# A windowed attention block with routed experts: the mask of the scores, the residual sum and the experts' gathers moved between PE, VectorE, GpSimd and the DMA queues

## The chip, the cores and the metric

The kernel runs on one core of one Trainium2 chip. The metric is the device time of one execution in microseconds (us). PE is the matmul engine (TensorE), DVE is VectorE, ACT is ScalarE, POOL is GpSimd, SP is SyncE, whose work here is to issue DMA transfers.

## The reference

`x` has shape (8, 512, 256), float32. The block computes `x + s * g`, with `xn` the layer norm of `x`:

```python
qkv = (xn @ qkv_w.T)                    # 32 heads of 8
attn = q @ k.T * 8**-0.5                # per head
m = (8 - |i - j| / 2) / 8 where i - 8 <= j < i + 8, else 0
attn = softmax(where(m != 0, attn * m, -inf))
s = (attn @ v) @ proj_w.T + proj_b
logits = xn @ router_w                  # 8 experts
e = argmax(logits); score = sigmoid(max(logits))
routed = (silu(score * xn @ gate_w[e]) * (score * xn @ up_w[e])) @ down_w[e]
shared = silu(xn @ shared_gate_w) * (xn @ shared_up_w) @ shared_down_w
g = silu(routed + shared)
out = x + s * g
```

## The kernel before

The 4096 tokens are 32 tiles of 128 rows (`T`). The whole work is one loop over steps n = 0 to `LAST` = 66, written out by hand once for each engine; each engine works through its own list in order, and semaphores join the lists. A step n < `U` = 64 is the attention of 64 queries (two blocks of 32) for all heads. Its parts lie in three steps: in step n PE makes the scores (`scores`, L902), DVE multiplies them by the distance weight out of PSUM into one of three buffers `Sx` (`weigh`, L711) and takes the row maximum (`largest`, L721), and GpSimd subtracts it (`subtract`, L422). In step n + 1 ACT takes the exponential (`exps`, L495) and DVE transposes the result in 32 x 32 blocks (`flipped`, L742). In step n + 2 PE multiplies by v (`weighted`, L930), DVE inverts the sums (`invert`, L751), ACT copies the result out (`o_out`, L500), and DVE divides and transposes (`divide`, `turned`). v goes through DRAM: SP writes it (`keep_v`) and reads it back, spread over partitions, as `VB` (`spread_v`, L318, four transfers for a step).

The mask is added by PE: `scores` first multiplies an identity by a bf16 table of 0 and -3e38 (L912), one matmul for each half of the channels, and then adds the scores to it in PSUM (L916). `mask_kind(n)` picks the table for the first, inner and last blocks of a sequence.

Other work is placed by step number. The shared expert takes steps 0 to 5 of each eight (`sg`, `su`, `sg`, `su`, `sd`, `sd` in `jobs_of`, L113); a step with `sg` is called a gate step in this text: in it DVE waits for ACT's tanh. Steps 8 to 10 do the routing, and from step 10 (`SENT`) to 16 GpSimd scatters five tiles of scaled rows a step to `xs_dram`, sorted by expert (L419). From step 18 (`E0`) to about 39 two tiles of 128 rows a step go through their expert (`expert_rows`, `expert_up`, `expert_down`, for DVE `gate` and `gated`), and the results go to `ys_dram`. The four PSUM banks `psM` are used in turn by all these jobs, in the order of `ORDER`.

From step 40 (`C_STEP`) on, the 4096 rows are put together in 16 chunks c of two tiles (`CT`, `NC`). GpSimd gathers a chunk's expert rows into one of three buffers Y (`gather`, L428: two indirect DMAs), three chunks ahead, and adds them to the shared expert's rows (`combine`, L440). ACT takes tanh (`silu`, L549), DVE finishes the silu (`silu`, L792), multiplies it with the attention's output (`result`, L803) and adds `x` (L806), which SP has loaded again into a buffer XR (`load_x`), and SP stores XR to `out` (`store`). `silu_at(n)` and `result_at(n)` give the chunks of a step: a chunk a step from 41 and 42 on until chunk 12 (steps 53 and 54), then chunks 13 (54, 58), 14 (61, 62) and 15 (62, 66).

In SP's list a step goes: stores and loads of x, blank rows of `xs_dram`, loads of expert rows, of weights, `keep_v`, `spread_v`.

## Time and profile before

| | us |
|---|---|
| median of 3 runs | 641.51 (639.12 to 642.87) |
| the profiled execution | 641.16 |
| its span, first to last instruction | 639.3 |

| engine | busy us | share of the span | instructions |
|---|---|---|---|
| PE | 562.8 | 88% | 3358 |
| DVE | 404.0 | 63% | 853 |
| ACT | 308.1 | 48% | 762 |
| POOL | 186.8 | 29% | 160 |

Busy time is the time in which an engine had an instruction in work; issuing a DMA from SP or ACT, waits and branches don't count, but GpSimd's indirect DMAs do, since GpSimd writes their descriptors itself. Matmuls are pipelined, and their ends are modelled: what one costs is better read from the distance between the starts of neighbours. A row of a timeline merges like instructions that follow each other (x2, x4); in brackets stands how long the engine was idle before, and what released it. A span average hides that each part of the loop has its own limit, so the stretches have to be read one by one.

### The profile page before, as it was taken

The page shows a single profiled execution, that of the slowest core. Times are in us where ns is not written, and L with a number is a line of the kernel's source. Part 1 is how long each engine was busy: PE and PEld are TensorE (multiplying, and loading weights), DVE is VectorE, ACT ScalarE, POOL GpSimd, SP SyncE. Part 2 cuts the span into 40 slices and gives each one's busy share as a digit, 9 for nine tenths or more (in the row PEclk, how much of TensorE's full clock was granted, in tenths as well). Part 3 has the DMA queues.
Part 4 walks back from the last instruction along what each step waited for, and adds up shares of the span by engine and source line. Part 5 has one row for each costly group of instructions (what it writes and reads, how often), then busy time and mean ns, then how long its engine had stood idle before and what let it go on. Part 6 is the DMA issues. An engine that isn't in the chain of part 4 may idle for free. (4 is left out here: it accounts for less than half of the span.)

```text
span 639.3 us, 10599 instructions
## 1 busy us (share of the span) xinstructions
PE 562.8 (88%) x3358; PEld 484.0 (76%) x3358; DVE 404.0 (63%) x853; ACT 308.1 (48%) x762; POOL 186.8 (29%) x160
## 2 busy tenths in 40 slices
PE   2879999969879999999999999999886868789865
PEld 1657888858757899898999898898775756677754
DVE  6655746886755455455455455456688888886773
ACT  1374654557773544543544634546454543635332
POOL 6000101147861011010010110014645545532230
PEclk9899999979998999999999999999989899989997
DMA  9415532112326667666567576443133333330110
GB/s 294 133 62 190 177 122 61 57 44 96 111 87 178 174 166 223 196 184 195 165 189 223 167 218 185 134 133 107 51 98 110 102 106 105 113 109 20 43 35 23
DMA packets 107370, 82.89 MB, mean 130 GB/s; under 512 B 42292, under 2 KB 104756, under 8 KB 107316
## 3 DMA queue, kind: packets, MB, share of 16 engines
q1 hardware_dynamic: 98628, 68.72, 36.6%
q0 software_dynamic: 3072, 8.39, 4.1%
q10 hardware_dynamic: 5616, 5.11, 2.3%
q8 instruction: 27, 0.44, 0.3%
q14 instruction: 27, 0.22, 0.1%
HBM read 59.12 MB, written 23.07 MB: 129 GB/s over the span
## 5 line engine op out<-in xcount | busy, mean ns | idle before, releaser
L425 POOL TENSOR_TENSOR Sx<-Sx,mx 128x752 f32<-128x752 f32 x64 | 93.7, 1464 | 414.9 <-DVE mx L725 414.8
L941 PE MATMUL psV<-VB,PTs 128*128 128x132 f32 x1024 | 137.3, 288 | 43.3 <-DMA VB<-v_dram 19.0
L941 PEld LDWEIGHTS psV<-VB,PTs 128*128 128x128 f32 x1024 | 130.1, 197 | 50.8 <-issue 50.0
L468 ACT ACTIVATE Or<-psV 32x128 f32<-32x128 f32 x256 | 68.5, 268 | 151.4 <-DVE rs L755 148.9
L916 PE MATMUL psS<-kBD,qBD 128*128 128x188 f32 x512 | 104.9, 329 | 0.0
L916 PEld LDWEIGHTS psS<-kBD,qBD 128*128 128x128 f32 x512 | 87.9, 195 | 10.8 <-issue 2.0
L747 DVE STREAM_TRANSPOSE PTs<-Sx 128x512 f32<-128x512 f32 x128 | 82.9, 685 | 1.0 <-ACT Sx L498 1.0
L991 PE MATMUL psM<-xT,EB 128*128 128x128 f32 x624 | 76.4, 276 | 0.0
L718 DVE TENSOR_TENSOR Sx<-psS,cst 128x752 f32<-128x752 f32 x64 | 59.7, 933 | 26.3 <-PE psS L916 26.2
L991 PEld LDWEIGHTS psM<-xT,EB 128*128 128x128 f32 x624 | 73.9, 192 | 2.1 <-ACT qBD L487 1.3
L732 DVE SCALAR_TENSOR_TENSOR ea<-et,psM 128x256 f32<-128x256 f32 x39 | 16.4, 421 | 76.3 <-PE psM L991 47.2
L968 PE MATMUL psM<-xnT,wsgu 128*128 128x512 f32 x128 | 63.1, 617 | 0.0
L725 DVE TENSOR_REDUCE mx<-Sx 128x16 f32<-128x752 f32 x64 | 59.9, 936 | 2.2
L468 ACT ACTIVATE kBD<-psM 32x272 f32<-32x272 f32 x128 | 49.2, 385 | 17.1 <-PE psM L898 15.9
L498 ACT ACTIVATE Sx<-Sx 128x752 f32<-128x752 f32 x64 | 53.0, 828 | 4.9 <-POOL Sx L425 4.5
L764 DVE TENSOR_TENSOR O<-Or,rs 128x128 f32<-128x128 f32 x64 | 23.6, 369 | 41.3 <-issue 38.5
L487 ACT ACTIVATE qBD<-psM,cst 128x512 f32<-128x512 f32 x64 | 38.7, 688 | 21.7 <-PE psM L893 21.6
L912 PE MATMUL psS<-maskb,identb 128*128 128x376 bf16 x128 | 42.0, 328 | 6.7 <-DVE Sx L718 3.9
L949 PE MATMUL psM<-wp,OT 128*128 128x256 f32 x128 | 33.7, 386 | 3.8 <-DVE OT L772 2.3
L1000 PE MATMUL psM<-EB,ehT 128*128 128x256 f32 x156 | 36.9, 379 | 0.0
L968 PEld LDWEIGHTS psM<-xnT,wsgu 128*128 128x128 f32 x128 | 23.3, 201 | 17.0 <-issue 16.9
L927 PE MATMUL psM<-wqkv,xnT 128*128 128x264 f32 x128 | 31.0, 390 | 5.6 <-DVE ag L779 2.8
(107 smaller groups left out, 690.6 us busy)
## 6 DMA issues: line engine op xcount, KB each, us to landing
EB<-in_L_ffn_gate_w SPq DMA_DIRECT2D x39, 256.0 KB, 3.0
EB<-in_L_ffn_up_w SPq DMA_DIRECT2D x39, 256.0 KB, 3.5
EB<-in_L_ffn_down_w SPq DMA_DIRECT2D x39, 256.0 KB, 3.1
VB<-v_dram SPq DMA_DIRECT2D x256, 32.0 KB
stage<-xs_dram SPq DMA_DIRECT2D x39, 128.0 KB, 2.2
ys_dram<-yb ACTq DMA_DIRECT2D x39, 128.0 KB, 3.1
xs_dram<-blank SPq DMA_DIRECT2D x9, 512.0 KB, 3.1
v_dram<-vS SPq DMA_DIRECT2D x8, 512.0 KB, 3.0
```

What stands on the lines that cost most here:

```text
L425: nc.gpsimd.tensor_tensor(s, s, mx[n % 3][:, :].unsqueeze(2).broadcast_to([P, 2 * G, KW]), ALU.subtract).then_inc(a_sub, 1)
L468: return nc.scalar.activation(dst, src, ACT.Copy)
L487: last = nc.scalar.activation(qBD[h % 2][:, :, :, i, :], q, ACT.Copy, scale=cst[:, C_HEAD + i:C_HEAD + i + 1])
L498: nc.scalar.activation(s, s, ACT.Exp).then_inc(a_exp, 1)
L718: tt(s, psS[:, :, 0:BW].rearrange("p j (g k) -> p j g k", k=KW), mw.unsqueeze(1).unsqueeze(1).broadcast_to([P, 2, G, KW]), ALU.mult).then_ ...
L725: reduce(mx[n % 3][:, :], Sx[n % 3][:, :, 0:KW], AX, ALU.max).then_inc(a_max, 1)
L747: last = nc.vector.transpose(PTs[n % 2][:, k, :, :, :].rearrange("p j i (r q) -> p (j i r) q", q=QB), Sx[n % 3][:, :, k * QB:(k + 1) * QB])
L912: mm(psS[:, j, 0:BW], identb[:, :], maskb[:, kind:kind + 2, :, :].rearrange("p i r k -> p (i r k)"), start=True, stop=False)
L916: last = mm(psS[:, j, i * HS * KW:(i + 1) * HS * KW], qBD[h % 2][:, j, k, :, :].rearrange("p s q -> p (s q)"), kBD[h % 2][:, j, :, k * QB: ...
L941: last = mm(psV[:, j, at:at + HS * VW], PTs[n % 2][:, k, j, i, :], VB[n % 2][:, i, k, :, VW * j:VW * j + VW], start=k == 0, stop=k == 1)
L968: last = mm(ps[:, :], wsgu[:, kc, at:at + P], xnT[:, b, kc, WIN:WIN + SEQ], start=kc == 0, stop=kc == KC - 1)
L991: last = mm(ps[:, f * P:(f + 1) * P], egu[:, i % 2, kc, f * P:(f + 1) * P], xT[:, i % 2, kc, :], start=kc == 0, stop=kc == KC - 1)
```

## The change

1. `masked_late(n)` is true for steps 0 to 7 and 18 to 63. In those, `scores` leaves the mask matmuls out, and GpSimd adds the mask to `Sx` in SBUF (`banded`), between `weigh` and `largest`. The table for it, 12 x 47 columns, is part of the constants loaded at the start. In those steps DVE's `largest(n)` moves behind `flipped(n-1)`.
2. `out` is set to `x` by eight transfers from DRAM to DRAM (`preset`, 512 KB each, steps 8 to 15). `load_x`, `store`, the buffers XR and DVE's addition are gone; GpSimd issues a transfer for each chunk that adds the product to `out` (`add_out`, 256 KB), a step after its `result`, the last one in step 66.
3. The gathers add straight to the shared expert's rows; `combine` is gone. `gather(c)` stands in the step before its `silu`, behind `subtract`, and waits for the shared rows; ACT's `silu` waits for the gather.
4. In SP's list `spread_v(n-1)` stands first in its step, from step 10 on.

```diff
--- before.py
+++ after.py
@@ -64,7 +64,8 @@
 C_M = C_ID + P
 C_BIAS = C_M + KW
 C_HEAD = C_BIAS + C
-C_STAY = C_HEAD + HS
+C_BAND = C_HEAD + HS
+C_STAY = C_BAND + 12 * KW
 C_TRI, C_ONE = C_STAY, C_STAY + P
 C_FIRST = C_ONE + P
 C_TILE = C_FIRST + E
@@ -89,6 +90,7 @@
     key = np.arange(KW)[None, :]
     kinds = (band & (key >= WIN), band, band, band, band, band & (key < QB + WIN))
     c[:, C_MASK:] = np.concatenate([np.where(k, 0.0, NEG) for k in kinds], 1)
+    c[:, C_BAND:C_STAY] = np.tile(c[:, C_MASK:].reshape(P, 3, 1, 2 * KW), (1, 1, KC, 1)).reshape(P, 12 * KW)
     return c
 
 
@@ -98,6 +100,10 @@
 
 def mask_kind(n):
     return 0 if n % UB == 0 else 2 if n % UB == UB - 1 else 1
+
+
+def masked_late(n):
+    return n < BATCH or n >= E0
 
 
 def first_key(n):
@@ -211,9 +217,9 @@
         at += NT * E
         rcst = EB[:, at:at + C_END - C_STAY]
         Y = [EB[:, i * CT * C:(i + 1) * CT * C] for i in range(3)]
-        XR = [EB[:, (3 + i) * CT * C:(4 + i) * CT * C] for i in range(3)]
 
         ident = cst[:, C_ID:C_ID + P]
+        band = cst[:, C_BAND:C_BAND + 12 * KW].rearrange("p (m k) -> p m k", k=KW)
         mw = cst[:, C_M:C_M + KW]
         bias = cst[:, C_BIAS:C_BIAS + C]
         tri = rcst[:, C_TRI - C_STAY:C_TRI - C_STAY + P]
@@ -238,15 +244,15 @@
             sem("r_" + n) for n in ("sc", "tanh", "sce", "oh", "cnt", "slot", "row", "tab"))
         r_scat = [sem(f"r_scat{i}") for i in range(SENDS)]
         m_full = [sem(f"m_full{i}") for i in range(MB)]
-        a_qk, a_S, a_mul, a_max, a_sub, a_exp, a_PT, a_V, a_PV, a_O, a_rec, a_nrm, a_OT, a_s = (
-            sem("a_" + n) for n in ("qk", "S", "mul", "max", "sub", "exp", "PT", "V", "PV", "O", "rec", "nrm", "OT", "s"))
+        a_qk, a_S, a_mul, a_add, a_max, a_sub, a_exp, a_PT, a_V, a_PV, a_O, a_rec, a_nrm, a_OT, a_s = (
+            sem("a_" + n) for n in ("qk", "S", "mul", "add", "max", "sub", "exp", "PT", "V", "PV", "O", "rec", "nrm", "OT", "s"))
         x_v, x_vd = ([sem(f"x_{n}{i}") for i in range(2)] for n in ("v", "vd"))
         f_tg, f_ag, f_hT, f_sh = (sem("f_" + n) for n in ("tg", "ag", "hT", "sh"))
         b_in, b_wd, b_st = ([sem(f"b_{n}{i}") for i in range(k)] for n, k in (("in", 4), ("wd", 2), ("st", 3)))
         b_wg = [sem(f"b_wg{i}") for i in range(2)]
         b_xT, b_et, b_ea, b_hT, b_y = (sem("b_" + n) for n in ("xT", "et", "ea", "hT", "y"))
-        d_y, d_x, d_st = ([sem(f"d_{n}{i}") for i in range(3)] for n in ("y", "x", "st"))
-        d_z, d_t, d_w, d_g, d_o = (sem("d_" + n) for n in ("z", "t", "w", "g", "o"))
+        d_y, d_st = ([sem(f"d_{n}{i}") for i in range(3)] for n in ("y", "st"))
+        d_t, d_w, d_g, d_pre = (sem("d_" + n) for n in ("t", "w", "g", "pre"))
 
         x_tiles = x.rearrange("(t p) c -> p t c", p=P)
         out_v = out.rearrange("(t p) c -> p t c", p=P)
@@ -350,24 +356,15 @@
                     full(sp, ("xa", i - 4))
                 sp.dma_start(stage[:, i % 4, :], xs_dram[i * P:(i + 1) * P, :]).then_inc(b_in[i % 4], 16)
 
-            def load_x(c):
-                b = c % 3
-                if c == 0:
-                    full(sp, ("xc", NX - 1))
-                if c >= 3:
-                    sp.wait_ge(d_st[b], 16 * (c // 3))
-                sp.dma_start(XR[b].rearrange("p (t c) -> p t c", t=CT), x_tiles[:, c * CT:(c + 1) * CT, :]).then_inc(d_x[b], 16)
-
-            def store(c):
-                b = c % 3
-                sp.wait_ge(d_o, c + 1)
-                sp.dma_start(out_v[:, c * CT:(c + 1) * CT, :], XR[b].rearrange("p (t c) -> p t c", t=CT)).then_inc(d_st[b], 16)
+            def preset(k):
+                rows = slice(k * NTOK // 8, (k + 1) * NTOK // 8)
+                sp.dma_start(out[rows, :], x[rows, :]).then_inc(d_pre, 16)
 
             for n in range(LAST + 1):
-                for c in result_at(n - 1):
-                    store(c)
-                    if c + 3 < NC:
-                        load_x(c + 3)
+                if BATCH < n - 1 < U:
+                    spread_v(n - 1)
+                if ROUTE <= n < ROUTE + 8:
+                    preset(n - ROUTE)
                 for i in range(2 * n - 4, 2 * n - 2):
                     if 0 <= i < 10:
                         fill(i)
@@ -387,13 +384,9 @@
                     load_weights(i)
                 if 0 <= n - 1 < BATCH:
                     keep_v(n - 1)
-                if 0 <= n - 1 < U:
+                if 0 <= n - 1 <= BATCH:
                     spread_v(n - 1)
-                if n == C_STEP:
-                    for c in range(3):
-                        load_x(c)
-            for c in result_at(LAST):
-                store(c)
+            sp.wait_ge(d_pre, 16 * 8)
             for b in range(3):
                 sp.wait_ge(d_st[b], 16 * len(range(b, NC, 3)))
 
@@ -419,6 +412,21 @@
                 pool.indirect_dma_start(xs_dram, bass.IndirectOffsetOnAxis(ap=slot[:, t:t + 1], axis=0),
                                         X[:, t, :], None).then_inc(r_scat[t // (T // SENDS)], 16)
 
+            def add_out(c):
+                pool.wait_ge(d_g, c + 1)
+                if c == 0:
+                    pool.wait_ge(d_pre, 16 * 8)
+                t = CT * c
+                pool.dma_start(out_v[:, t:t + CT, :], S0[:, t:t + CT, :] if t < EARLY else X[:, t:t + CT, :],
+                               accum_op=ALU.add).then_inc(d_st[c % 3], 16)
+
+            def banded(n):
+                pool.wait_ge(a_mul, n + 1)
+                s = Sx[n % 3][:, :, :].rearrange("p (m r) k -> p m r k", r=HS)[:, :, :, 0:KW]
+                kind = 2 * KC * mask_kind(n)
+                nc.gpsimd.tensor_tensor(s, s, band[:, kind:kind + 2 * KC, :].unsqueeze(2).broadcast_to([P, 2 * KC, HS, KW]),
+                                        ALU.add).then_inc(a_add, 1)
+
             def subtract(n):
                 pool.wait_ge(a_max, n + 1)
                 s = Sx[n % 3][:, :, 0:KW]
@@ -426,28 +434,20 @@
                                         ALU.subtract).then_inc(a_sub, 1)
 
             def gather(c):
-                b = c % 3
                 if c == 0:
                     for k in range(3):
                         pool.wait_ge(b_st[k], 16 * len(range(k, NX, 3)))
-                if c >= 3:
-                    pool.wait_ge(d_w, c - 2)
+                pool.wait_ge(f_sh, c + 1)
                 for k in range(CT):
                     t = c * CT + k
-                    pool.indirect_dma_start(Y[b][:, k * C:(k + 1) * C], None, ys_dram,
-                                            bass.IndirectOffsetOnAxis(ap=slot[:, t:t + 1], axis=0)).then_inc(d_y[b], 16)
-
-            def combine(c):
-                b = c % 3
-                z = shared_rows(c * CT).rearrange("p t c -> p (t c)")
-                pool.wait_ge(d_y[b], 16 * CT * (c // 3 + 1))
-                pool.wait_ge(f_sh, c + 1)
-                nc.gpsimd.tensor_tensor(z, Y[b], z, ALU.add).then_inc(d_z, 1)
+                    pool.indirect_dma_start(shared_rows(c * CT)[:, k, :], None, ys_dram,
+                                            bass.IndirectOffsetOnAxis(ap=slot[:, t:t + 1], axis=0),
+                                            compute_op=ALU.add).then_inc(d_y[c % 3], 16)
 
             for n in range(LAST + 1):
-                for c in silu_at(n):
-                    combine(c)
                 if n < U:
+                    if masked_late(n):
+                        banded(n)
                     subtract(n)
                 if n == SENT:
                     pool.wait_ge(s_fill, 16 * 10)
@@ -455,12 +455,12 @@
                 for t in range((n - SENT) * SPS, min((n - SENT + 1) * SPS, T)):
                     if t >= 0:
                         scatter(t)
-                if n == C_STEP:
-                    for c in range(3):
-                        gather(c)
-                for c in silu_at(n - 1):
-                    if c + 3 < NC:
-                        gather(c + 3)
+                for c in silu_at(n + 1):
+                    gather(c)
+                for c in result_at(n - 1):
+                    add_out(c)
+            for c in result_at(LAST):
+                add_out(c)
 
         @block.scalar
         def _(act):
@@ -547,7 +547,9 @@
                 act.dma_start(ys_dram[i * P:(i + 1) * P, :], yb[:, i % 3, :]).then_inc(b_st[i % 3], 16)
 
             def silu(c):
-                act.wait_ge(d_z, c + 1)
+                act.wait_ge(d_y[c % 3], 16 * CT * (c // 3 + 1))
+                if c >= 3:
+                    act.wait_ge(d_w, c - 2)
                 z = shared_rows(c * CT).rearrange("p t c -> p (t c)")
                 nc.scalar.activation(Y[c % 3], z, ACT.Tanh, scale=0.5).then_inc(d_t, 1)
 
@@ -719,7 +721,10 @@
                    mw.unsqueeze(1).unsqueeze(1).broadcast_to([P, 2, G, KW]), ALU.mult).then_inc(a_mul, 1)
 
             def largest(n):
-                dve.wait_ge(a_mul, n + 1)
+                if masked_late(n):
+                    dve.wait_ge(a_add, len([k for k in range(n + 1) if masked_late(k)]))
+                else:
+                    dve.wait_ge(a_mul, n + 1)
                 if n >= 3:
                     dve.wait_ge(a_sub, n - 2)
                 reduce(mx[n % 3][:, :], Sx[n % 3][:, :, 0:KW], AX, ALU.max).then_inc(a_max, 1)
@@ -796,14 +801,11 @@
                 stt(z, Y[b], 1.0, z, ALU.add, ALU.mult).then_inc(d_w, 1)
 
             def result(c):
-                b, t = c % 3, CT * c
+                t = CT * c
                 s = (S0[:, t:t + CT, :] if t < EARLY else X[:, t:t + CT, :]).rearrange("p t c -> p (t c)")
                 dve.wait_ge(a_s, CT * c + CT)
                 dve.wait_ge(d_w, c + 1)
                 stt(s, shared_rows(t).rearrange("p t c -> p (t c)"), 0.5, s, ALU.mult, ALU.mult).then_inc(d_g, 1)
-                dve.wait_ge(d_x[b], 16 * (c // 3 + 1))
-                dve.wait_ge(d_g, c + 1)
-                tt(XR[b], s, XR[b], ALU.add).then_inc(d_o, 1)
 
             moments(0)
             variance(0)
@@ -820,7 +822,8 @@
             for n in range(LAST + 1):
                 if n < U:
                     weigh(n)
-                    largest(n)
+                    if not masked_late(n):
+                        largest(n)
                 if n == 0:
                     variance(1)
                     deviation(1)
@@ -836,6 +839,8 @@
                     table()
                 if 0 <= n - 1 < U:
                     flipped(n - 1)
+                if n < U and masked_late(n):
+                    largest(n)
                 for i in pair_at(n, 1)[:1]:
                     gate(i)
                     gated(i)
@@ -901,7 +906,8 @@
 
             def scores(n):
                 h, u = divmod(n, UH)
-                if n == 0:
+                late = masked_late(n)
+                if n == BATCH:
                     pe.wait_ge(s_cast, 2)
                 if n >= 1:
                     pe.wait_ge(a_mul, n)
@@ -909,12 +915,13 @@
                     pe.wait_ge(a_qk, 3 * h + 3)
                 kind = 2 * mask_kind(n)
                 for j in range(KC):
-                    mm(psS[:, j, 0:BW], identb[:, :], maskb[:, kind:kind + 2, :, :].rearrange("p i r k -> p (i r k)"),
-                       start=True, stop=False)
+                    if not late:
+                        mm(psS[:, j, 0:BW], identb[:, :], maskb[:, kind:kind + 2, :, :].rearrange("p i r k -> p (i r k)"),
+                           start=True, stop=False)
                     for i in range(2):
                         k = block_of(n, i) % (HALF // QB)
                         last = mm(psS[:, j, i * HS * KW:(i + 1) * HS * KW], qBD[h % 2][:, j, k, :, :].rearrange("p s q -> p (s q)"),
-                                  kBD[h % 2][:, j, :, k * QB:k * QB + KW], start=False, stop=i == 1)
+                                  kBD[h % 2][:, j, :, k * QB:k * QB + KW], start=late, stop=late or i == 1)
                 last.then_inc(a_S, 1)
 
             def values(t):
```

## Rows read from the trace of the kernel before

**Rows 1.** Stretches: length; busy us (instructions) per engine; clock; DMA share; GB/s.

```profile
29.00:116.00 87.00, 80.29 (x439) 66.82 (x438) 54.53 (x117) 46.34 (x111) 12.19 (x8) 1.00 0.37 120
116.00:188.00 72.00, 63.53 (x351) 52.04 (x350) 49.26 (x112) 47.56 (x118) 44.60 (x41) 0.95 0.23 73
188.00:441.00 253.00, 249.13 (x1665) 224.75 (x1665) 132.49 (x285) 116.93 (x305) 33.31 (x23) 0.99 0.60 177
441.00:570.00 129.00, 102.91 (x558) 84.25 (x557) 103.14 (x177) 61.42 (x144) 70.09 (x61) 0.95 0.35 102
570.00:639.00 69.00, 53.34 (x311) 44.89 (x309) 45.49 (x99) 27.83 (x71) 15.99 (x11) 0.92 0.14 36
```

**Rows 2.** PE's waits, 188 to 441 us: total, times, longest.

```profile
PE psV L941 <- DMA VB<-v_dram: 3.5, 1, 3.5
```

**Rows 3.** PE's timeline, one step's scores: start, length, instruction.

```profile
254.40 0.32 PE L912 MATMUL psS<-maskb,identb 128*128 128x376 bf16 x1
254.56 0.80 PE L916 MATMUL psS<-kBD,qBD 128*128 128x188 f32 x4
...
256.00 0.59 PE L893 MATMUL psM<-xnT,wqkv 128*128 128x256 f32 x2
```

**Rows 4.** Timeline around step 18, SP and PE.

```profile
189.89 1.80 SPq L327 DMA_DIRECT2D VB<-v_dram  x4
...
193.10 1.16 PE L941 MATMUL psV<-VB,PTs 128*128 128x132 f32 x8 [3.53 <-DMA VB<-v_dram]
```

**Rows 5.** DVE's timeline, a step without a result.

```profile
595.14 0.93 DVE L718 TENSOR_TENSOR Sx<-psS,cst 128x752 f32<-128x752 f32 x1
...
598.18 0.24 DVE L755 RECIPROCAL rs<-psV 128x8 f32<-128x8 f32 x2
...
600.22 0.90 DVE L718 TENSOR_TENSOR Sx<-psS,cst 128x752 f32<-128x752 f32 x1
```

**Rows 6.** Groups by line: busy us, mean ns, idle before.

```profile
L425 POOL TENSOR_TENSOR Sx<-Sx,mx 128x752 f32<-128x752 f32 x64 | 93.7, 1464 | 414.9 <-DVE mx L725 414.8
...
L445 POOL TENSOR_TENSOR xnT<-EB,xnT 128x512 f32<-128x512 f32 x14 | 18.2, 1303 | 3.7 <-ACT xnT L468 3.5
```

**Rows 7.** Timeline of one step of the combination, DVE and GpSimd.

```profile
482.57 0.94 DVE L718 TENSOR_TENSOR Sx<-psS,cst 128x752 f32<-128x752 f32 x1
...
484.56 1.45 POOL L425 TENSOR_TENSOR Sx<-Sx,mx 128x752 f32<-128x752 f32 x1 [3.26 <-DVE mx L725]
...
487.43 0.95 POOL L437 DMA_INDIRECT EB<-ys_dram,slot  x1 [0.31 <-issue]
...
488.22 2.00 DVE L803 SCALAR_TENSOR_TENSOR X<-xnT,X 128x512 f32<-128x512 f32 x1
488.40 1.27 POOL L445 TENSOR_TENSOR xnT<-EB,xnT 128x512 f32<-128x512 f32 x1
...
490.33 0.69 DVE L806 TENSOR_TENSOR EB<-X,EB 128x512 f32<-128x512 f32 x1
490.94 0.94 DVE L718 TENSOR_TENSOR Sx<-psS,cst 128x752 f32<-128x752 f32 x1
```

**Rows 8.** GpSimd's timeline: its subtract in steps 40, 41, 42, 43 and 55.

```profile
441.25 1.45 POOL L425 TENSOR_TENSOR Sx<-Sx,mx 128x752 f32<-128x752 f32 x1 [3.59 <-DVE mx L725]
...
451.42 1.45 POOL L425 TENSOR_TENSOR Sx<-Sx,mx 128x752 f32<-128x752 f32 x1
...
457.94 1.45 POOL L425 TENSOR_TENSOR Sx<-Sx,mx 128x752 f32<-128x752 f32 x1 [3.86 <-DVE mx L725]
...
467.83 1.45 POOL L425 TENSOR_TENSOR Sx<-Sx,mx 128x752 f32<-128x752 f32 x1 [4.78 <-DVE mx L725]
...
570.48 1.45 POOL L425 TENSOR_TENSOR Sx<-Sx,mx 128x752 f32<-128x752 f32 x1 [3.76 <-DVE mx L725]
```

**Rows 9.** DVE's last instructions.

```profile
635.29 0.69 DVE L803 SCALAR_TENSOR_TENSOR X<-xnT,X 128x512 f32<-128x512 f32 x1
```

**Rows 10.** DMA issues: KB, median us from issue to landing.

```profile
EB<-ys_dram,slot POOLq DMA_INDIRECT x32, 2.8
```

## The prediction

> **What bounds the kernel now.** I read the stage table first. From 188 to 441 us (steps 17 to 40, experts under way) PE is busy 249.13 of 253 us at granted clock 0.99, while DVE is busy 132.49: PE sets the pace [rows 1]. In the list of waits of that stretch PE has one long wait, 3.5 us for VB [rows 2]; everything else that is late there is late beside PE. From 441 to 570 us (steps 41 to 54, the final combination) DVE is busy 103.14 of 129 us and PE 102.91 [rows 1]; the timeline of one step shows DVE working without a gap except a wait for ACT, so there it is DVE's order that counts [rows 7]. From 570 to 639 us no engine is over 80% busy [rows 1], yet the steps follow each other on DVE's in-order list [rows 5]. From 29 to 116 us PE is busy 80.29 of 87 us [rows 1]. Steps 10 to 16 are paced by GpSimd's scatters and keep their mask on PE, so I change nothing there.
>
> A program's own time was 641.16 us in the profiled run, against a span of 639.3 and a median of 641.51; I sum against 641.16, which is 0.35 below the median.
>
> **The mask off PE (54 of 64 steps).** A step's scores are two mask matmuls and eight passes of L916. The first mask starts at 254.40, what follows it at 254.56: 0.16 us each, although the busy column says 0.32, since ends are modelled. The whole block is 1.60 us and becomes 1.28 [rows 3]. Per step 0.32 us.
> Steps 19 to 39 are PE's: 21 x 0.32 = -6.7. The cover for everything else there is DVE's slack of 120 us in 253 [rows 1]; without it, this gain is gone.
> Steps 0 to 7: 8 x 0.32 = 2.6 at most, nothing at least, since part of those steps is a chain through DVE; I take -1.0.
>
> **The mask on GpSimd.** No row shows this instruction. The nearest are L425 (752 elements, one input repeated from 16 values, 1.464 us) and L445 (512 elements, both inputs read in full, 1.303) [rows 6]. The new one reads both inputs in full over 752 elements: L445's undisturbed 1.27 [rows 7] x 752 / 512 = 1.87. Between 1.46 and 1.87 I take 1.85.
> The Trainium skill, "GPSIMD Engine Reference", section 3.1, speaks against moving elementwise work here: about 2.6 cycles per element for two inputs, which at the page's 1.2 GHz is an estimate of 1.63 us plus dispatch for 752 elements. The sum by that estimate would be some 3 us lower than by mine.
>
> DVE's order in a late step becomes weigh, flipped(n-1), then largest, which waits for GpSimd. In a bare step now invert (L755) starts 598.18 - 595.14 = 3.04 us after weigh (L718), and the step takes 600.22 - 595.14 = 5.08 [rows 5]. After: 0.94 (weigh) + 0.08 (semaphore) + 1.85 + 0.06 + 0.94 (largest) = 3.87, less 0.03 of overlap: 3.84. So +0.80 us for a step whose pace is DVE's. Queued behind the waiting largest are gate, gated, invert, divide; ACT's copies of Or and PE's next experts wait for those.
>
> **Step 18.** SP's spread of v now stands first in a step, so spread_v(16) is no longer behind the wait for the scatters. Now it is issued at 189.89 and PE starts on it at 193.10, after 3.53 us [rows 4]. DVE's own step (5.08 + 0.80 + 1.52 for a gate step, see below) lets only part through: -2.5, between 0 and -3.5.
>
> **Steps 40 and 41.** Now six gathers stand in a row in front of subtract(41): 10.17 us from 441.25 to 451.42, and 6.52 to 457.94 [rows 8]. After, one pair per step. A gate step on DVE is 5.08 + 0.80 + 1.52 = 7.4, where 1.52 is the gate step's 9.89 (457.94 to 467.83) [rows 8] less the common 8.37 (482.57 to 490.94) [rows 7]: -2.8. Step 41 by GpSimd's list (6.75, below) +0.2. Together -2.6.
>
> **Steps 42 to 54** last 570.48 - 457.94 = 112.54 us [rows 8]. DVE's common step of 8.37 loses the second result instruction (0.61 from 490.33 to 490.94) and, with GpSimd's combine (488.40, 1.27 us) gone, L803 goes from 2.11 to 0.69, which it takes when GpSimd is idle [rows 7, 9]: 8.37 - 0.61 - 1.42 + 0.80 = 7.14.
> GpSimd's list becomes: mask 1.85, wait for largest 0.06 + 0.94 + 0.08, subtract 1.45, two gathers (from subtract's end at 486.01 to 488.38, 2.37) [rows 7], then the add to out: 0.3 gap plus D. That is 7.05 + D. The next mask stands behind it, and DVE's largest behind that.
> D, a direct accumulating transfer of 256 rows, is in no row. The nearest is a gather of 128 rows, 0.95 [rows 7]. If that is a cost per instruction, D is 1.0; if per row, 1.9. Since the index must be looked up for each row of a gather and not here, I take 1.0.
> So 8.05 per step, bound by GpSimd, and 7.14 + 1.52 = 8.66 in the three gate steps. Step 54 has no gather: 5.08 + 0.80 + 0.69 = 6.6. Sum 9 x 8.05 + 3 x 8.66 + 6.6 = 105.0: -7.5.
> ACT now waits for the gather itself: the second one starts 5.8 us after the mask's start (4.38 and 487.43 - 486.01), lands 2.8 us later [rows 10], tanh 0.63, so 9.2; ACT's copy behind it is wanted at 8.05 + 1.85 + 1.27 = 11.2. Covered by 2.0 us; an accumulating gather that lands over 2 us later than a plain one uses that up.
> The preset's eight transfers (8 MB read and written in all) lie in steps 8 to 15, where DMA is busy 0.23 [rows 1]: nothing.
>
> **Steps 55 to the end.** Nine steps x 0.80 = +7.2; results 13 to 15 lose 0.7 each, -2.1; gathers 14 and 15 now stand in steps 60 and 61, where GpSimd's 0.08 + 6.75 + wait for the shared rows exceeds DVE's step, +2.2. At the end, now L803 ends at 635.98 and the span 3.3 us later, with the add and a store [rows 9]; after, D 1.0 plus a landing of 2.8 or more: +0.7. Sum +8.0. This part is a loss.
>
> Total: -6.7 - 1.0 - 2.5 - 2.6 - 7.5 + 8.0 = -12.3, so 628.9, given as 629.
>
> **The rivals.**
> Cheap GpSimd (0.10): the mask costs 1.46 as L425 does. Steps 42 to 54 and 55 on each lose about 3.5 less: 622.
> Exposed largest (0.12): in steps 19 to 39 the wait for the mask delays gate and gated, and PE's 6.7 is not seen: 636. For it: in rows 5 the order is tight. Against it: DVE idles half of that stage.
> Transfer by rows (0.16): D = 1.9. Then the list is 8.95 in all twelve steps, +9.0, and about 1 more after step 54: 639, no change that can be told.
> GpSimd's queue becomes the bound and eats everything (0.22): D, or the accumulating gathers, cost more than a plain row shows. Every us of D above 1.6 is 12 us between steps 42 and 54, and a us or two in the rest. From D = 2.1 on the kernel is slower than before; at D = 2.6 it is 648. For it: GpSimd's list holds four kinds of work there, one of a kind the trace has never seen. Against it: all its 64 transfers took about 1 us.
> Forecast (0.40): 629.
> That the change doesn't do what it says is part of the second rival: the masks go, the time stays.
>
> **How the numbers follow.** This kernel can be told from no change at about 0.5%, 3.2 us. Faster: 0.40 + 0.10 + 0.12 = 0.62. Same: 0.16. Slower: 0.22. The range goes from the cheap case with step 18's full gain, 618, to a D of about 2.5, 646.
>
> **What would show it.** Right: L912 20 times instead of 128, DVE's bare step near 5.9, GpSimd's steps near 8.05 between 42 and 54 with a direct transfer of about 1.0, L803 at 0.7 throughout, no wait for VB at step 18, PE still without waits from 200 to 430 us. Wrong: a direct transfer over 2 us, waits of L732 or L991 for DVE in the expert stage, ACT's L552 waiting for DMA so long that Or comes late, or gathers well above 1 us.

## The result

The changed kernel took 651.45 us (median of 4 runs, 649.36 to 651.69), the kernel before 640.91 beside it. The ratio is 1.0149, 95% interval [1.0117, 1.018]: slower by some 10 us, or 1.5%, where a gain of 12 was forecast. The profiled execution has a span of 649.7 us against 639.3.

The same five stretches as [rows 1], now of the kernel after (length, then busy us and instructions of each engine, TensorE's clock, DMA share, GB/s):

```profile
29.00:116.00 87.00, 80.90 (x442) 67.88 (x441) 57.59 (x130) 49.09 (x117) 25.25 (x17) 1.00 0.41 132
116.00:188.00 72.00, 61.85 (x344) 51.20 (x343) 49.07 (x105) 46.66 (x115) 44.74 (x41) 0.95 0.41 124
188.00:441.00 253.00, 249.76 (x1669) 226.06 (x1667) 135.48 (x293) 123.72 (x322) 79.15 (x51) 1.00 0.61 176
441.00:570.00 129.00, 95.02 (x469) 79.37 (x470) 73.82 (x150) 52.84 (x122) 99.86 (x65) 0.88 0.48 65
570.00:639.00 69.00, 52.78 (x285) 45.11 (x283) 41.36 (x92) 27.61 (x71) 36.37 (x24) 0.88 0.23 36
```

Up to 441 us PE is about as full as before. From 441 to 570 DVE fell from 103.14 to 73.82 us of work, as wanted, and GpSimd rose from 70.09 to 99.86: it is now the fullest engine there. PE's mean clock of 0.88 in that stretch, 0.95 before, came with less work on PE (95.02 us for 102.91). The clock does not set the common step: a kernel further down (mask_all) has the same 0.88 there and a common step 1.3 us shorter.

The start of GpSimd's subtract in single steps is the ruler of what follows; the common step is the distance from one to the next in a step without a gate or another extra job. Before, from [rows 8] and the same view: step 40 at 441.2, 42 at 457.9, 55 at 570.5, 63 at 621.2, span 639.3. After: 430.2, 446.3, 570.8, 627.9, 649.7.

| Part | Before, us | After, us | Change | Forecast |
|---|---|---|---|---|
| to step 40 | 441.2 | 430.2 | -11.0 | -10.2 |
| 40 to 42 | 16.7 | 16.1 | -0.6 | -2.6 |
| 42 to 55 | 112.6 | 124.5 | +11.9 | -7.5 |
| 55 to 63 | 50.7 | 57.1 | +6.4 | with the next: |
| 63 to the end | 18.1 | 21.8 | +3.7 | +8.0 for both |

Of the miss of 22.7 us, 19.4 lie in steps 42 to 54. One of them, the counterpart of [rows 7] (timeline of the kernel after; start, length, engine, line, the wait before it and its releaser in brackets; ... stands for lines left out):

```profile
478.97 2.79 POOL L427 TENSOR_TENSOR Sx<-Sx,cst 128x752 f32<-128x752 f32 x1
481.40 0.63 ACT L554 ACTIVATE EB<-xnT 128x512 f32<-128x512 f32 x1 [5.17 <-DMA xnT<-ys_dram,slot]
481.80 0.94 DVE L730 TENSOR_REDUCE mx<-Sx 128x16 f32<-128x752 f32 x1 [2.94 <-POOL Sx L427]
...
482.81 1.45 POOL L433 TENSOR_TENSOR Sx<-Sx,mx 128x752 f32<-128x752 f32 x1 [1.05 <-DVE mx L730]
482.95 1.11 ACT L468 ACTIVATE Or<-psV 32x128 f32<-32x128 f32 x4 [0.93 <-DVE rs L760]
...
484.21 3.44 PE L948 MATMUL psV<-VB,PTs 128*128 128x132 f32 x16 [4.61 <-ACT Or L468]
...
484.41 1.68 POOL L443 DMA_INDIRECT xnT<-ys_dram,slot  x1 [0.15 <-issue]
...
485.69 0.68 DVE L808 SCALAR_TENSOR_TENSOR X<-xnT,X 128x512 f32<-128x512 f32 x1
...
486.39 1.56 POOL L443 DMA_INDIRECT xnT<-ys_dram,slot  x1 [0.30 <-issue]
...
487.37 1.91 POOL L420 DMA_DIRECT2D out<-X  x1
...
488.16 2.81 POOL L427 TENSOR_TENSOR Sx<-Sx,cst 128x752 f32<-128x752 f32 x1
```

GpSimd has no idle time but the 1.05 us for the largest and 0.45 us that the profile calls issue. L427 is the mask (1.65 us when GpSimd is free at its start; the 2.79 shown overlap the transfer before it), L433 the subtract, L443 the two accumulating gathers, L420 the add to out. The step, mask start to mask start, is 488.16 - 478.97 = 9.19 us: mask 1.65, wait 1.05, subtract 1.45, and 5.04 for the three transfers with their gaps. The forecast had 8.05, with 3.67 for the transfers. DVE now waits 2.94 us for the mask and ACT 5.17 for the gather. L808 is at 0.68, as forecast.

The waits of that stretch, 441 to 570 us (total, times, longest):

```profile
ACT EB L554 <- DMA xnT<-ys_dram,slot: 58.5, 12, 6.1
...
DVE mx L730 <- POOL Sx L427: 29.3, 14, 3.8
PE psV L948 <- ACT Or L468: 25.6, 12, 4.6
...
DVE O L769 <- issue: 18.7, 11, 3.9
```

### The profile page after: what moved, and what is told of

The parts are those of the page before. It is cut to its first block and busy times, and to the rows that moved or that the text cites. A ratio compares the mean times of both kernels' runs of the same rounds, so it can differ in the third digit from the quotient of the medians.

```text
span 649.7 us, 10380 instructions
## 1 busy us (share of the span) xinstructions
PE 553.4 (85%) x3250; PEld 480.1 (74%) x3250; DVE 379.0 (58%) x837; ACT 308.0 (47%) x762; POOL 298.9 (46%) x214
## 5 line engine op out<-in xcount | busy, mean ns | idle before, releaser
L427 POOL TENSOR_TENSOR Sx<-Sx,cst 128x752 f32<-128x752 f32 x54 | 101.8, 1886 | 214.3 <-DVE Sx L720 214.3
L948 PE MATMUL psV<-VB,PTs 128*128 128x132 f32 x1024 | 145.6, 299 | 48.7 <-ACT Or L468 48.2
L948 PEld LDWEIGHTS psV<-VB,PTs 128*128 128x128 f32 x1024 | 137.8, 208 | 57.1 <-issue 56.3
L433 POOL TENSOR_TENSOR Sx<-Sx,mx 128x752 f32<-128x752 f32 x64 | 93.2, 1456 | 96.0 <-DVE mx L730 95.8
L923 PE MATMUL psS<-kBD,qBD 128*128 128x188 f32 x512 | 94.5, 325 | 4.6 <-ACT kBD L468 3.5
L923 PEld LDWEIGHTS psS<-kBD,qBD 128*128 128x128 f32 x512 | 84.6, 191 | 13.6 <-DVE Sx L720 4.0
L720 DVE TENSOR_TENSOR Sx<-psS,cst 128x752 f32<-128x752 f32 x64 | 59.5, 930 | 18.1 <-PE psS L923 18.0
L443 POOL DMA_INDIRECT xnT<-ys_dram,slot x28 | 46.3, 1652 | 12.2 <-ACT xnT L468 6.5
L769 DVE TENSOR_TENSOR O<-Or,rs 128x128 f32<-128x128 f32 x64 | 19.8, 310 | 46.0 <-issue 46.0
L903 PE MATMUL psM<-xnT,wqkv 128*128 128x272 f32 x128 | 35.8, 404 | 9.7 <-ACT qBD L487 9.7
L554 ACT ACTIVATE EB<-xnT 128x512 f32<-128x512 f32 x14 | 8.8, 630 | 69.9 <-DMA xnT<-ys_dram,slot 69.9
```

The costliest lines, as they stand in the source:

```text
L427: nc.gpsimd.tensor_tensor(s, s, band[:, kind:kind + 2 * KC, :].unsqueeze(2).broadcast_to([P, 2 * KC, HS, KW]), ALU.add).then_inc(a_add, 1)
L433: nc.gpsimd.tensor_tensor(s, s, mx[n % 3][:, :].unsqueeze(2).broadcast_to([P, 2 * G, KW]), ALU.subtract).then_inc(a_sub, 1)
L443: pool.indirect_dma_start(shared_rows(c * CT)[:, k, :], None, ys_dram, bass.IndirectOffsetOnAxis(ap=slot[:, t:t + 1], axis=0), compute_op= ...
L720: tt(s, psS[:, :, 0:BW].rearrange("p j (g k) -> p j g k", k=KW), mw.unsqueeze(1).unsqueeze(1).broadcast_to([P, 2, G, KW]), ALU.mult).then_ ...
L923: last = mm(psS[:, j, i * HS * KW:(i + 1) * HS * KW], qBD[h % 2][:, j, k, :, :].rearrange("p s q -> p (s q)"), kBD[h % 2][:, j, :, k * QB: ...
L948: last = mm(psV[:, j, at:at + HS * VW], PTs[n % 2][:, k, j, i, :], VB[n % 2][:, i, k, :, VW * j:VW * j + VW], start=k == 0, stop=k == 1)
```

## The experiments

Fifteen kernels. They come from four parts of the change and one edit that is not in it:

- M, the mask on GpSimd; O, the preset of out and the accumulating adds to it; G, the accumulating gathers without GpSimd's separate add; S, the earlier spread of v.
- the tanh late: ScalarE's tanh of the combination stands behind its copies of the step (q, k, Or), not ahead of them.

A part undone means that the lines marked - in the diff stand again for those marked +; M undone is `return False` in masked_late.

**The accumulating transfers, made plain.** The gathers overwrite; the shared expert's part of the output is left out:

```diff
-  ap=slot[:, t:t + 1], axis=0), compute_op=ALU.add).then_inc(d_y[c % 3], 16)
+  ap=slot[:, t:t + 1], axis=0)).then_inc(d_y[c % 3], 16)
```

> The changed kernel, but its gathers overwrite the shared expert's rows instead of adding to them (the shared expert is missing from the output); places, waits and bytes read are the same. Theory (the price of the accumulating transfers on GpSimd's list is what eats the gain between steps 42 and 54): a gather goes back from 1.6 us to about 0.96 on GpSimd and its landing from 4.0 to about 2.8, the steps there go from 9.2 to about 7.9 us, and the kernel from 651 to about 638. Rival (the place of the gathers, right behind subtract and in front of ACT's tanh, is what costs, whatever they do): under 4 us of gain, 647 to 651.

635.61 us, ratio to before 0.9918 [0.9894, 0.9943]: 16 us below the full change and near the 638 of the theory. The same with the add to out (`accum_op=ALU.add` gone, so x is missing in the output):

> The changed kernel, but the products are written to out instead of added to it (x is missing from the sum). Theory: the 1.9 us of the add on GpSimd are mostly the price of any direct transfer of 256 rows, so the steps gain 0 to 0.5 us each; the landing falls from 5.3 us to about 2.5, and with it the kernel's end: 643 to 647. Rival (accumulating to DRAM is itself the dear part): the issue falls to about 1.0, 12 steps gain 0.9 each, and with the end the kernel comes to about 637.

646.47 us, 1.0088 [1.0061, 1.0115]: 5 us below the full change, inside the theory's range. The groups by line from 441 to 570 us, after first, then with plain gathers, then with the plain store:

```profile
L443 POOL DMA_INDIRECT xnT<-ys_dram,slot x24 | 39.6, 1652 | 9.8 <-issue 4.8 <-ACT xnT L468 4.6
...
L420 POOL DMA_DIRECT2D out<-X x10 | 18.4, 1837 | 0.0
```

```profile
L443 POOL DMA_INDIRECT xnT<-ys_dram,slot x24 | 25.9, 1080 | 8.6 <-issue 4.7 <-ACT xnT L467 3.5
...
L420 POOL DMA_DIRECT2D out<-X x11 | 15.0, 1365 | 0.0
```

```profile
L420 POOL DMA_DIRECT2D out<-X x11 | 14.0, 1275 | 0.0
```

An accumulating gather holds GpSimd 1.65 us, a plain one 1.08; the add to out 1.84, plain 1.28. The common step went from 9.2 to 8.1 with plain gathers and to 8.6 with the plain store: 1.1 and 0.6 us. The two savings are not independent. The add to out, untouched in the first of these kernels, fell to 1.37 us beside plain gathers, and about half of the 1.1 us is that. No run here has both plain.

Against the forecast of 3.67 the three transfers take 1.37 us more. From the end of the subtract to the start of the add to out, the gathers take 487.37 - 484.26 = 3.11 us, forecast 2.37: 0.74. The add has the other 1.93, forecast 1.3 with its gap: 0.63. So it is the accumulating forms of both that were priced too low, the gathers as much as the D I had argued about.

**The adds to out alone undone.** SP loads x, DVE adds, SP stores, as before; M, G and S stay:

> The changed kernel with the output as in the kernel before (x loaded again, added by DVE, stored by SP; no preset, no adding transfers of GpSimd). Theory: GpSimd's list in a step of 42 to 53 loses 2.2 us (9.2 to 7.0), DVE's is 7.14 + 0.61 = 7.75 and sets the pace, 12 steps give about 1.3 us each, the end 5: 631 to 634. Rival (the gathers alone, through ACT's wait, keep the steps at 9): 644 to 647.

647.39 us, 1.0087 [1.0059, 1.0115]: a miss by 13. The total is within 0.4 us of the rival's, though its common step of 9 is not there: the common step did fall to 8.1, but steps 44, 48, 52 and 53 took 11.9, 13.2, 12.7 and 10.2. Shortening GpSimd's list by a transfer did not help where something else was late.

**The mask taken back to steps before 40.** Its one edit:

```diff
 def masked_late(n):
-    return n < BATCH or n >= E0
+    return n < BATCH or E0 <= n < C_STEP
```

> The changed kernel with the mask on GpSimd only in steps 0 to 7 and 18 to 39; from step 40 on it is PE's again, and largest stands ahead of flipped. Theory (GpSimd's list is the bound there): 1.65 us of mask and the wait for largest leave the list, the steps of 42 to 53 go from 9.2 to about 7 us, the later ones lose about 0.5 each: 612 to 622. Rival (ACT's wait for the gathers is the bound, the list is not): the steps stay at 8.5 or more, 640 to 645.

631.02 us, 0.9834 [0.979, 0.9878]. A gain of 20 us over the change, and yet 9 above what I expected: the common steps fell to 6.2 to 6.5, but 44, 48, 52 and 53 took 10.1 to 12.3. The same mask on the kernel before, with the earlier spread of v and the old transfers:

> The kernel before with the mask on GpSimd in steps 0 to 7 and 18 to 39 only and with spread_v first in SP's steps; output, gathers and combine as before. Theory (up to step 40 the forecast held: the trace after is 11.0 us earlier at the subtract of step 40, and all of it is the mask and SP's order): 630. Rival (part of the lead came from the transfers that this kernel takes back, such as the loads of x): 633 to 637.

627.03 us, 0.9787 [0.9748, 0.9827]. That is 3 us better than the theory's 630. Its steps from 42 to 55 take 112.6 us, the same as before; 13.5 of the 14.5 us between the two profiled spans lie ahead of the subtract of step 40. This also rules out the exposed largest in the expert stage: steps 20 to 38 take 216.6 us there, 223.6 before.

**What makes the long steps.** In the trace of the change, step 52, lines of ACT, GpSimd and DVE:

```profile
538.35 0.63 ACT L554 ACTIVATE EB<-xnT 128x512 f32<-128x512 f32 x1 [5.17 <-DMA xnT<-ys_dram,slot]
539.01 2.42 ACT L487 ACTIVATE qBD<-psM,cst 128x512 f32<-128x512 f32 x4
539.04 0.94 DVE L730 TENSOR_REDUCE mx<-Sx 128x16 f32<-128x752 f32 x1 [2.95 <-POOL Sx L427]
...
540.05 1.45 POOL L433 TENSOR_TENSOR Sx<-Sx,mx 128x752 f32<-128x752 f32 x1 [1.05 <-DVE mx L730]
541.31 1.57 ACT L468 ACTIVATE kBD<-psM 32x272 f32<-32x272 f32 x4
...
542.90 1.11 ACT L468 ACTIVATE Or<-psV 32x128 f32<-32x128 f32 x4
544.03 0.60 ACT L468 ACTIVATE xnT<-psM 128x512 f32<-128x512 f32 x1
544.10 0.29 DVE L769 TENSOR_TENSOR O<-Or,rs 128x128 f32<-128x128 f32 x1 [3.94 <-issue]
...
544.90 2.03 POOL L443 DMA_INDIRECT xnT<-ys_dram,slot  x1 [3.40 <-ACT xnT L468]
```

ACT stands 5.17 us at L554 for a gather to land. Behind it wait the copies of q (2.42) and k (1.57), the copy Or for which DVE stands 3.94 (the profile calls this wait issue, but L769 starts 0.09 us after the copy's end), and the copy of the shared rows for which GpSimd's next gather stands 3.40. So the wait comes round to GpSimd, and the step takes 12.8 us. The forecast asked only when Or is wanted, the copy that follows the tanh in a common step; these 4 us stand between the two here. The edit that tests it:

```diff
-                for c in silu_at(n):
-                    silu(c)
 ...
                 if 0 <= n - 2 < U:
                     o_out(n - 2)
+                for c in silu_at(n):
+                    silu(c)
```

> The changed kernel with one move: ACT's tanh of a chunk (its silu, which waits for the gather) stands behind its copy of the attention's output in the step instead of ahead of the q and k copies. Theory (two parts of loss: GpSimd's list gives the common step of 9.2, and ACT's wait for the gather holds back the q and k copies and Or in steps 44, 48, 52 and 53, which take 9.8 to 12.8): those four steps fall to about 9.2 to 9.5, together -6, 645. Rival (those long steps are PE's or DVE's own work for the shared expert and the projections): 650 to 652.

645.84 us, 1.0081 [1.0039, 1.0122]. That is the theory's 645, from the move of one instruction. Steps 44 to 51 are now 9.2 each without exception, which is GpSimd's list, and steps 42 to 53 take 112.7 us for 117.2. Steps 52 and 53 still take 10.4 and 10.7, where 9.2 to 9.5 was expected: in each, GpSimd's gather waits 1.35 us for ACT's copy of the shared rows. The same with the mask ended at step 39:

> The kernel whose mask is on GpSimd only in steps 0 to 7 and 18 to 39, with ACT's tanh moved behind its copy of the attention's output. Theory (with the mask off GpSimd's list, ACT's wait ahead of the q and k copies was what kept it at 631: steps 44, 48, 52 and 53 took 11.1, 12.3, 12.1 and 10.1 us, the others 6.2 to 8.5): those fall to 7 to 8.5, -12 to -16, 615 to 619. Rival (DVE now waits for the tanh in every step instead): 626 to 632.

**610.29 us**, 0.9507 [0.9471, 0.9543], faster than the kernel before by 5%, than the change by 6%, and by 5 us more than I expected. The waits of 441 to 570 us in it:

```profile
ACT Or L468 <- DVE rs L760: 54.2, 15, 5.4
POOL Sx L433 <- DVE mx L730: 32.7, 10, 7.0
...
ACT EB L554 <- DMA xnT<-ys_dram,slot: 2.4, 2, 1.4
```

ACT's 58.5 us at the gather are 2.4 now. The common steps take 6.3 to 6.7: the list without the mask and its wait is 1.45 + 5.04 = 6.5. Of the 32.7 us for which GpSimd waits for the largest, 7.6 lie ahead of 533 us, where step 55 starts; in its common steps there is no such wait. Then out stored in the old way in that kernel:

> As the run before (mask on GpSimd only in steps 0 to 7 and 18 to 39, ACT's tanh late, gathers that add), but with the output as in the kernel before: x loaded again, added by DVE, stored by SP. Theory: GpSimd's list loses 2.2 us a step, DVE's gains 0.6, so the common step is DVE's 7.0; the end is 5 us shorter, since SP's store is over 2.5 us after its issue and GpSimd's 8 us: 610 to 615. Rival (the loads of x and the stores hold up the loads of v in SP's list again): 620 or more.

617.11 us, 0.9615 [0.9589, 0.9641], 2 us over the bound I gave. Common step 7.1, near the 7.0 expected for DVE's list with its second result instruction. So there the accumulating store is worth 7 us, in spite of its tail.

**The tail.** The kernel of 610.29 us with only its last chunk added by DVE and stored by SP (the load of that chunk's x and DVE's addition are not shown):

```diff
             sp.wait_ge(d_pre, 16 * 8)
+            sp.wait_ge(d_o, 1)
+            sp.dma_start(out_v[:, (NC - 1) * CT:NC * CT, :], XL.rearrange("p (t c) -> p t c", t=CT)).then_inc(d_last, 16)
 ...
-            for c in result_at(LAST):
-                add_out(c)
```

> The changed kernel with the mask on GpSimd only up to step 39, ScalarE's tanh of the combination behind its output copies, and the last chunk of out alone handled as before the change: x loaded, VectorE adds, SyncE stores. Theory (a last transfer issued by GpSimd ends the span 7 to 8 us after its issue, SyncE's store 2.5 us after the last add): the run of the same kernel without this edit gave 610.3 us with 7.8 us from issue to end; here 610.3 - 7.8 + 0.7 (one more add of DVE) + 2.5 = about 605.5. Rival (the tail is the time in which all of GpSimd's earlier transfers drain, and goes with them): 609 to 611.

**606.25 us**, 0.9449 [0.9425, 0.9474], the fastest of all, and within 1 us of the 605.5 expected. The last transfer of the full change (span 649.7), and of this kernel (span 606.1):

```profile
641.74 1.23 POOL L420 DMA_DIRECT2D out<-X  x1 [11.18 <-DVE X L808]
```

```profile
603.57 0.40 SPq L395 DMA_DIRECT2D out<-EB  x1
```

8.0 us from issue to the end of the span against 2.5. With the plain store on GpSimd's queue (o_plain) it was still 7.0 us. So most of the tail goes with the engine that issues the last transfer, not with accumulation.

**The parts alone.** M alone on the kernel before, in all late steps:

> The kernel before with the mask on GpSimd outside steps 8 to 17 and nothing else of the change. Theory (the mask is a gain up to step 40 and a loss behind 55, and it was the transfers' prices that made 42 to 55 grow): step 40 about 9 to 12 us earlier, common step of 42 to 54 from GpSimd's list 1.65 + 1.45 + 1.3 + 2 x 0.95 and about 1.5 of gaps = 7.8 to 8.6 (8.4 before), so -5 to +3; 55 to the end +5 (5.6 for 5.0 in the bare steps); total about 632 to 638. Rival (the late masks alone carry the loss): common step over 9, total above 641.

645.13 us, 1.006 [1.0044, 1.0077]: the rival's total, though not by its common step. The common step fell to 7.9, which is the sum of the list (1.65 + 1.05 + 1.45 + 3.75 for two plain gathers and the add), but the even steps took 9.3 to 11.6, 42 to 55 took 118.3, and 40 to 42 took 19.7 where it was 16.7. So my new theory, that the transfers' prices alone made the loss, fell here. O, G and S without M:

> The changed kernel with all masks on TensorE: only the preset and accumulating stores, the accumulating gathers and the earlier spread of V are left. Theory: front -2 (step 18 alone), GpSimd's common cycle 9.19 - 1.65 = 7.5 us, so the step falls from 8.4 to about 7.7 (9 x -0.7 = -6), steps in which ScalarE's q and k copies stand behind the tanh +2 to +3 each (4 of them, +8 to +11), the end +5: 641 - 2 - 6 + 8 to 11 + 5 = 646 to 649. Rival (without the mask the list has room enough that ScalarE's wait is covered again): 637 to 640.

640.02 us, 0.9987 [0.9972, 1.0002], no change that can be told: the rival's total, but by neither's way. The long steps stayed (11.0, 12.3 and 11.9 for 44, 48 and 52), and the common step fell to 6.2, where I had 7.7, since with the mask its wait for the largest goes from the list too. M, O and S without G:

> The changed kernel with the gathers and the separate add on GpSimd of the kernel before (gathers three chunks ahead); mask, preset and accumulating stores, and earlier spread of V stay. Theory: common list 1.65 + 1.45 + 1.3 (the add) + 2 x 0.95 + 1.9 (add to out) = 8.2 and gaps, 8.7 to 9.2 us, no wait of ScalarE for a fresh gather, so steps 44, 48, 52 and 53 at 9 to 10.5; end +5: 642 to 648. Rival (the accumulating gather is the whole loss): below 638.

654.06 us, 1.0208 [1.019, 1.0225], the slowest of all and outside both: GpSimd's list has both the separate add and the add to out, 9.3 us in the common step.

**The order of the tanh with the old transfers.** Three controls:

> The kernel before with one edit: ScalarE's tanh of the combination stands behind its copies of q, k and of the output instead of ahead of them; nothing of the change. Theory (the tanh's wait, 18.8 + 4.9 us of ScalarE's time between 441 and 570 us behind GpSimd's add, delays the copies in the kernel before too): the common step falls from 8.4 towards 7.5, total 628 to 636. Rival (the kernel before is bound there by VectorE and its waits beside GpSimd, and the order of ScalarE does not matter until the change makes the wait long): 639 to 643.

639.83 us, 0.9981 [0.9959, 1.0004]. The rival: nothing.

> The kernel before with the mask on GpSimd outside steps 8 to 17, old gathers and stores, and ScalarE's tanh behind its copies. Theory (the long steps 44, 46, 48, 50, 52 of mask_all, 9.3 to 11.6 us, are ScalarE's wait ahead of the copies; without it GpSimd's list of 7.9 us is all): steps 42 to 54 take 13 x 8 and a little = 105 to 109 us where mask_all took 118.3, total 632 to 637. Rival (the late mask lengthens the chain of one step itself, through the largest): total over 640.

646.84 us, 1.0102 [1.0068, 1.0137]. The rival again: steps 42, 48 and 50 are 11.6, where the kernel before has 9.9.

> The kernel before with the mask on GpSimd up to step 39 outside 8 to 17, the earlier spread of V, and ScalarE's tanh behind its copies; old gathers, add and stores. It differs from the fastest kernel so far (610.3 us) by the accumulating transfers alone, and from one that gave 627.0 by ScalarE's order alone. Theory (the accumulating transfers are a gain of some us once the tanh is late, as they take the add from GpSimd and from VectorE): 614 to 622. Rival (they are worth nothing, the order is all): 608 to 611.

627.88 us, 0.9794 [0.9762, 0.9825]. Outside both, above the 614 to 622 of the theory: the accumulating transfers are a gain with the tanh late, as it said, but of 17.6 us where it had 4 to 12.

Put together, medians in us (a star: without S, which is about 3 of the difference, since step 40 starts at 433.2 with M alone and at 430.2 in the full change):

| | old transfers | accumulating |
|---|---|---|
| mask to step 39, tanh early | 627.0 | 631.0 |
| mask to step 39, tanh late | 627.9 | 610.3 |
| mask in late steps too, tanh early | 645.1* | 651.45 |
| mask in late steps too, tanh late | 646.8* | 645.8 |

The kernel before, run beside each round, had medians from 640.9 to 642.5 us, so a difference of 2 us between two cells can't be told from none. Read by rows and columns: the late mask costs 15 to 36 us in every pair. The accumulating transfers (O and G together) lose 4 and 9 us with the tanh early (with the star's 3 allowed for), make no difference that can be told with the late mask and the tanh late, and gain 17.6 in the fourth cell, where neither the mask nor the tanh stands in their way. The tanh's place is worth nothing that can be told with the old transfers, and 5.6 and 20.7 us with the accumulating ones. None of these is a price that could be added to another; each is what is left when the latest thing in a step is taken away.

## Why the prediction was wrong

**Mask off PE, step 18: right in its main part, and in part by luck.** To step 40 it forecast -10.2, and -11.0 came. M alone had step 40 at 433.2, -8.0 against a forecast of -7.7; S and the preset add -3.0, forecast -2.5. In the stretch 188 to 441 us PE is busy 249.76 of 253 and the largest waits there beside it. From the subtract of step 19 to that of step 40 the trace has -6.2, forecast -6.7; in the whole kernel the mask's matmul is left 20 times, as said. But steps 0 to 7 gave -3.7, where the prediction had -1.0 and called 2.6 the most; why is open. What hid it is the ruler: from step 18 on a subtract waits for its mask, which puts its start 1.7 us later (step 17 to 18 takes 6.8 us for 5.0) at no cost in total; the forecast had no term for that. And S, the preset and the accumulating transfers without the mask (no_M) have step 40 5.2 us earlier, so the two gains do not add up either.

**The price of the mask: 1.85 forecast, 1.65 measured.** I scaled from L445 and was high. The bare step rose from 5.0 to 5.6 us, not 5.9, so nine steps from 55 on cost 5.0 us instead of 7.2. From the Trainium skill's "GPSIMD Engine Reference", section 3.1, the prediction had an estimate of 1.63 us plus dispatch; the trace agrees within 0.02, which leaves next to nothing for dispatch. By the same figure the 512 elements of L445 would be an estimate of 1.11 us, where [rows 6] has 1.30, so one agreement says little of how far the rule reaches.

**Steps 42 to 54: the failed step, 19.4 us.** The prediction's step of 8.05, GpSimd's list with plain prices and ACT covered behind it, failed in three terms. First the list, 9.19 instead of 8.05: over twelve steps 13.7 us. In it the mask is 0.2 cheaper, and the transfers 1.37 dearer. The argument on D looked only at the add to out; that the gathers change from a plain to an accumulating form was named in a rival and had no term in the sum. Second, "covered by 2.0 us". The landing of a gather went from 2.8 [rows 10] to 4.0 us, and the gather starts later in the longer list: of the cover 0.93 us is left in a common step, ACT's wait at Or in the timeline above. In the steps with q and k copies up to 4 us more stand behind the tanh, which is not covered. Steps 42 to 53 take 117.2 us, 6.8 more than twelve times 9.2 (48 has 11.1, 52 has 12.8, 53 has 10.5); 1.8 of these I had as gate steps, so 5.0 of the miss. With the tanh late 2.4 of the 6.8 are left, all in steps 52 and 53. Third, step 54 took 7.3, not 6.6. Sum 19.4.

The fourth rival, GpSimd's queue as the bound, is what happened. By its own price a list of 9.19 is D = 2.14, which it put at the point where the gain is gone, some 641. Most of the other 10 us is ACT's lateness (5.0) and the tail (4.3 over its term), and the rival had neither. Two of the prediction's signs of being wrong came: gathers well above 1 us, and the tanh waiting for DMA so long that Or comes late. A direct transfer over 2 us did not: D was 1.9.

**Steps 40 and 41:** -0.6 instead of -2.6. Step 41 takes 8.2 us, forecast 6.75, from the same list: with plain gathers it is 6.55. The rest is step 40, 7.8 for 7.4, which plain gathers do not change.

**The end:** +0.7 forecast. L808 ends at 641.43, and the span 8.3 us later, where it was 3.3 [rows 9]: +5.0. I had taken a landing of a gather in mid-kernel for a last transfer on the same queue. The two steps with gathers, 60 and 61, rose by 5.9, forecast 3.8. The cheaper mask in the other steps, and 1.3 us less from the subtract of step 63 to the last result, offset most of this, so the part came to +10.1 against +8.0: that it is near is luck.

**What the late mask does where GpSimd is not full** is in part open. In mask_all with the tanh late the gate steps grew from 9.9 to 11.6, by 1.7 us, while a bare step grew by 0.6. The largest holds up DVE's reciprocal, and with it ACT's Or, tg and DVE's gate behind tg. The prediction named gate, invert and Or as queued behind it, without a price. No run splits the 1.7.

## What to carry to other kernels

An in-order engine with four kinds of work is priced by the sum of its list, and every instruction of a new form in it needs its own price: here the plain rows were a lower bound. When a wait on one engine is replaced by a direct wait on a transfer, list all that stands behind it on that engine, step by step, not in the common step alone. And costs of parts that share one step do not add: a 2 x 2 of the parts showed a gain of 17.6 us that no single removal had shown; here the accumulating transfers are good, and the late mask and the early tanh are what spoils them.

## What the chip showed that was not expected

An accumulating gather of 128 rows holds GpSimd 1.65 us against 1.08 for a plain one in the same list, and lands after 4.0 us against 2.8 in the kernel before, where it goes to another buffer (no landing of a plain gather is on record in the changed kernels). An accumulating transfer of 256 rows of 1 KB from GpSimd holds it 1.84 to 1.92 us beside accumulating gathers, 1.37 to 1.40 beside plain ones and 1.23 alone at the end; a plain one takes 1.28 beside accumulating gathers and 0.76 alone. So its price depends on what was issued ahead of it. The transfers by kind in the kernel after (KB each, median us to landing):

```profile
out<-X POOLq DMA_DIRECT2D x14, 256.0 KB, 5.3
...
xnT<-ys_dram,slot POOLq DMA_INDIRECT x28, 4.0
```

A kernel whose last transfer GpSimd issues ended 7.0 to 8.2 us after the issue, in eight kernels (7.0 with the plain store, 7.8 to 8.2 with the accumulating one); with SP's store 2.5 us.
